# TensorE's order in a two-layer transformer kernel: products moved within both cross attentions, the second attention and the first experts

## The chip, the core and the metric

The kernel runs on one core of a Trainium2 chip. The core's engines are TensorE (PE; PEld is its weight load), VectorE (DVE), ScalarE (ACT), GpSimd (POOL) and SyncE (SP, which here only starts transfers). Each follows its own list of instructions and waits on semaphores for the others. The metric is the device time of one execution in microseconds; fewer is better.

## The reference

Eight sequences of 100 tokens with 256 channels pass through two layers. `ctx` has 361 rows per sequence; gates are tanh of one number each.

```python
# layer 0
x = x + tanh(g_xattn[0]) * cross_attention_0(layernorm(x), ctx)   # 16 heads of 64; query i sees the keys j with j % 100 == i
x = x + tanh(g_ffn[0]) * block_0(layernorm(x))                     # self attention, then experts, each with a residual
# layer 1
x = x + tanh(g_xattn[1]) * cross_attention_1(layernorm(x), ctx)   # 16 heads of 16, all keys
x = x + tanh(g_ffn[1]) * experts_1(layernorm(x))                   # 8 experts, best 2 of the distances to 8 centroids

def block_0(x):
    x = x + attention(rmsnorm(x))          # causal, 16 heads, latent keys of 32, rotated half
    p = softmax(rmsnorm(x) @ Wgate + bias) # 8 experts, best 2, weights normed
    return x + shared(rmsnorm(x)) + sum_e comb[:, e] * (silu(x@Wg[e]) * (x@Wu[e])) @ Wd[e]
```

Where accuracy asks for it, the kernel splits a float32 factor in a high part (rounded to fp32r) and the low rest, and adds three products: high by high, high by low, low by high.

## The kernel before

All is written out by hand, one function per engine; the order of an engine's instructions is the order of the Python loops. Tokens stand in columns, in two halves of 400 (four sequences each). PS is the PSUM, eight banks; `mm` (line 501) issues nearly every product of PE, so nearly all rows of PE name L501.

**First cross attention.** For each sequence b, `keys(b)` makes eight key tiles and `values(b - 1)` eight value tiles, six fp32r products each (`project_a`). DVE multiplies keys by queries (`products`, L1753), PE sums heads (`sim`), DVE and ACT make the softmax in six steps (`softmax_a`, L1761 to L1780, with `exps`, L1168, and `round_weights`, L1175, on ACT). Behind each value tile but ahead of the next, PE spreads the softmax weights over the tile's rows (SPREAD by SES); ACT copies the values (`vcopy`, L1185), DVE weighs them (`weigh`, L1792), POOL adds the keys' slots (L1529, L1532). The eight sums behind it are `project_out_a`, four groups of 24 products: one stands between `values(6)` and `values(7)`, three follow.

**Second attention.** 16 steps (8 sequences by 2 groups of heads): scores (`qk`), a softmax by DVE and ACT with POOL, transposes (`turn`, L672), the mixed values (`mix`) and ACT's copies of them (L1264). Then four groups of four float32 products, (half n, channels mo), project the output; each adds 1 to `b_output_summed`, and DVE adds it to Y (L1888). They read UT and WOA.

**First experts.** `norm(3)`, the router's scores (float32, 8 columns), then nine expert tiles by two halves, 18 steps: `up(i)` makes gate and up sides, six products each; ACT takes SiLU (L1292), DVE multiplies (`gate_up`, L1987) and weighs by the router's weight (L2006), ACT and DVE split the hidden part (HTH L1332, HTL L1963), `down(i)` makes six products. ACT rounds the weights of a tile (`split_hi0`, L1282), DVE takes the rest (`split_lo0`, L1952). The router's chain of some 20 short steps runs on DVE. Its result is transposed (L770) into WTS, spread over all rows by 16 products with UNIT, and copied out of four banks by ACT (even, L1321) and DVE (odd, L1994).

**Second cross attention.** The keys of a sequence are stored to HBM and come back head by head (KST). The queries are turned into that order by `stack_queries(n)` for half n, 16 products with PICK into three banks that ACT (`stack_even`, L1397) and DVE (`stack_odd`, L2071) empty. The loop over q from -2 to 32 has four steps of heads g per sequence b: scores (KST by QST), DVE's maxima (L2087), the transposed scores (QST by KST, 3 pieces), exps on ACT (L1369), `mix_v` (24 small products), and pieces of `project`, which makes later sequences' keys and values. In two places products on the weights alone stand ahead of `mix_v`: `fold_output` (eight float32 products with 8 columns or 1) at b = 4, g = 0, and `fold_centroids` (four such products, WO1T by the centred centroids, which DVE has made in the same step) at b = 5, g = 0; DVE reads both after the last step of that b.

**Second experts** follow with tokens sorted by expert; nothing in them is touched.

## Time and profile before

| what | value |
|---|---|
| three runs | 808.63, 802.99, 808.98 us (median 808.63) |
| profiled execution | 809.94 us, its span 808.1 us |
| mean granted clock of PE | 0.946 of full |
| PE busy | 724.1 us (90%) |
| DVE, ACT, POOL busy | 504.1, 380.6, 237.0 us |
| moved from and to HBM | 74.74 and 10.38 MB |

The span is the time from the first to the last instruction of the profiled execution, and the 1.8 us more lie around it. Busy times of engines overlap. The granted clock is the share of full speed that PE's clock had: 1.00 is 2.4 GHz, 0.50 is 1.2 GHz.

### The profile page before, as it was taken

The numbers are of one execution on the slowest core, as the hardware profiler recorded it, in microseconds if no ns is written. First come the engines' busy times: TensorE is split into PE (matmuls) and PEld (weight loads), VectorE is DVE, ScalarE is ACT, GpSimd is POOL, SyncE is SP. The second block draws the span as 40 slices with busy tenths as digits, with TensorE's granted clock in tenths as the row PEclk, the third lists the DMA queues.
The fourth block names the chain that finished last, engine by engine and source line by source line (L and its number), as shares of the span: only waits on it lengthen the run. The fifth ranks groups of instructions, "written<-read, shape, count | busy, mean of one in ns | idle before, by whom it ended". The sixth has DMA issues, their size and how long they took to land.

```text
span 808.1 us, 13459 instructions
## 1 busy us (share of the span) xinstructions
PE 724.1 (90%) x4735; PEld 603.7 (75%) x4735; DVE 504.1 (62%) x998; ACT 380.6 (47%) x828; POOL 237.0 (29%) x254
## 2 busy tenths in 40 slices
PE   6999999998989289989998899989994699999996
PEld 3578888888955178658996467667773699999995
DVE  3366666665339979537665666776786376665652
ACT  4513233322352169735434356665575256555561
POOL 0006655556205424600003402111200223243232
PEclk9999999999999789797999999998897599999999
DMA  6500000000060000000000776653233468999972
GB/s 236 212 2 20 18 20 20 18 2 0 15 270 1 0 1 2 2 1 0 1 10 1 170 150 167 144 134 95 84 141 125 135 217 307 306 328 295 327 219 58
DMA packets 30001, 85.97 MB, mean 106 GB/s; under 512 B 3913, under 2 KB 20425, under 8 KB 26609
## 3 DMA queue, kind: packets, MB, share of 16 engines
q1 hardware_dynamic: 26097, 79.88, 30.5%
q0 software_dynamic: 3840, 5.25, 3.1%
q8 instruction: 39, 0.64, 0.3%
q14 instruction: 25, 0.20, 0.1%
HBM read 74.74 MB, written 10.38 MB: 105 GB/s over the span
## 4 chain that ended last, share of the span: by engine, by line
PE 54%; DVE 12%; issue 4%; DMA 3%; ACT 2%; POOLq 0%; SPq 0%; DVEq 0%; ACTq 0%
PE PS L501 50%; DVE SM L2087 2%; PE PS L1073 2%; DVE WK L1849 1%; PE PS L672 1%; DVE WK L1846 1%; DMA XB<-token_rows,XROW 1%; DMA KST<-mask_rows 1%; DVE KTHL L2050 1%; PE PS L1043 1%; PE PS L889 1%; ACT RO L1246 0%; DMA out<-YO,TROW 0%; ACT SQ L1118 0%; DMA keys_by_head<-KTHL 0%
## 5 line engine op out<-in xcount | busy, mean ns | idle before, releaser
L501 PE MATMUL PS<-CTXH,WKV0H 128*128 128x362 f32 x256 | 87.1, 340 | 3.9 <-DVE PROD L1753 3.3
L2087 DVE TENSOR_REDUCE SM<-PS 100x1 f32<-100x362 f32 x128 | 64.5, 530 | 37.7 <-PE PS L501 36.9
L501 PE MATMUL PS<-CTXL,WKV0H 128*128 128x362 f32 x256 | 84.5, 330 | 0.0
L501 PE MATMUL PS<-CTXH,WKV0L 128*128 128x362 f32 x256 | 84.5, 330 | 0.0
L1369 ACT ACTIVATE WK<-PS 120x400 f32<-120x400 f32 (+1 forms) x96 | 48.3, 508 | 44.5 <-PE PS L501 43.6
L1792 DVE TENSOR_TENSOR RW<-PS,RW 128x400 f32<-128x400 f32 x64 | 36.8, 575 | 48.7 <-ACT RW L1185 32.9
L1185 ACT COPY RW<-PS 128x361 f32<-128x361 f32 x64 | 29.6, 463 | 66.8 <-PE PS L501 51.5
L1649 POOL DMA_INDIRECT out<-YO,TROW x20 | 31.7, 1583 | 100.0 <-DMA out<-YO,TROW 50.2
L501 PE MATMUL PS<-KST,QST 97*100 97x362 f32 x128 | 53.1, 425 | 7.9 <-DVE SM L2087 3.7
L501 PEld LDWEIGHTS PS<-CTXH,WKV0H 128*128 128x128 f32 x256 | 48.6, 190 | 12.9 <-DVE PROD L1753 6.6
L501 PE MATMUL PS<-RB,HTT 114*128 114x256 f32 (+1 forms) x240 | 55.2, 379 | 0.6 <-ACT HTT L1481 0.6
L1529 POOL TENSOR_TENSOR RW<-RW 128x200 f32<-128x200 f32 x64 | 39.4, 616 | 52.2 <-DVE RW L1792 49.8
L2150 DVE TENSOR_TENSOR GUL<-RB,GUH 128x1368 fp32r<-128x1368 f32 x28 | 44.2, 1578 | 14.3 <-ACT GUH L1407 14.3
L501 PE MATMUL PS<-GUH,XTH 128*128 128x342 f32 x160 | 51.7, 323 | 0.0
L501 PE MATMUL PS<-GUL,XTH 128*128 128x342 f32 x160 | 51.7, 323 | 0.0
L501 PE MATMUL PS<-GUH,XTL 128*128 128x342 f32 x160 | 51.6, 323 | 0.0
L1613 POOL TENSOR_TENSOR QST<-QALL,COLS 96x800 fp32r<-96x800 f32 x15 | 22.9, 1546 | 94.3 <-PE PS L501 84.8
L501 PEld LDWEIGHTS PS<-RB,HTT 114*128 114x128 f32 (+1 forms) x240 | 44.7, 189 | 6.2 <-ACT HTT L1481 0.9
L501 PEld LDWEIGHTS PS<-CTXL,WKV0H 128*128 128x128 f32 x256 | 49.1, 192 | 0.0
L501 PEld LDWEIGHTS PS<-CTXH,WKV0L 128*128 128x128 f32 x256 | 48.7, 190 | 0.0
L1753 DVE TENSOR_TENSOR PROD<-PS,RQ 128x400 f32<-128x400 f32 x64 | 36.4, 571 | 12.1 <-PE PS L501 11.2
L2310 DVE TENSOR_TENSOR STD<-PS,SIL 128x342 f32<-128x342 f32 x40 | 20.5, 511 | 32.2 <-PE PS L501 32.2
(328 smaller groups left out, 1863.0 us busy)
## 6 DMA issues: line engine op xcount, KB each, us to landing
RB<-W SPq DMA_DIRECT2D x14, 1368.0 KB, 5.9
RB<-W SPq DMA_DIRECT2D x20, 768.0 KB, 7.1
KST<-keys_by_head SPq DMA_DIRECT2D x24, 362.0 KB
RQ<-W SPq DMA_DIRECT2D x6, 1368.0 KB, 6.0
keys_by_head<-KTHL SPq DMA_DIRECT2D x8, 724.0 KB, 3.6
CTX<-ctxT SPq DMA_DIRECT2D x16, 361.0 KB, 6.5
RW<-WGU SPq DMA_DIRECT2D x1, 2304.0 KB, 8.5
RW<-WKV SPq DMA_DIRECT2D x1, 2048.0 KB, 9.9
```

The lines of the kernel that those rows point to most:

```text
L501: return pe.matmul(out, lhsT, rhs, start=start, stop=stop)
L1073: m = pe.transpose(PS[0:HT1, 5 + j, x * P:(x + 1) * P], H1T[:, j, x * HT1:(x + 1) * HT1], IDN[:, :])
L1185: act.copy(VSB[:, i % 3, 0:KV], PS[:, 4 + i % 2, 0:KV]).then_inc(sem["a_values_copied"], 1)
L1369: act.activation(PTC[0:CHT[c], q % 2, c, :], PS[0:CHT[c], 2 + c, 0:4 * S], ACT.Exp).then_inc(sem["c_exp_taken"], 1)
L1529: pool.tensor_tensor(pv[:, 0:2 * S], pv[:, 0:2 * S], pv[:, 2 * S:4 * S], ALU.add).then_inc(sem["a_halves_added"], 1)
L1613: pool.tensor_tensor(QST[b % 3][0:96, :, u, :], QALL[0:96, :, tok(b)].bitcast(F32), COLS[0:96, 21 + u:22 + u].unsqueeze(2).to_broadcast([9 ...
L1649: pool.indirect_dma_start(t["out"], bass.IndirectOffsetOnAxis(ap=TROW[:, k:k + 1], axis=0), YO[:, k % 2, :], None, compute_op=ALU.add).the ...
L1753: dve.tensor_tensor(out, k, q, ALU.mult).then_inc(sem["a_products_ready"], 1)
L1792: dve.tensor_tensor(PV[:, i % 3, :], PS[:, 6 + i % 2, 0:HALF], VSB[:, i % 3, :], ALU.mult).then_inc(sem["a_weighted"], 1)
L2087: dve.tensor_reduce(SM1[:, q % 2, j:j + 1], PS[0:S, i % 2, 0:KVE], AX_X, ALU.max, negate=True).then_inc(sem["c_maximum_found"], 1)
L2150: dve.tensor_tensor(GUL[k % 2][:, :, j, :], raw_gu(k, j), GUH[k % 2][:, :, j, :], ALU.subtract).then_inc(sem["expert_weights_low_ready"], 1)
L2310: dve.tensor_tensor(H1T[:, j, :], PS[:, 2 * j + 1, 0:HH], SIL1[:, j, :], ALU.mult).then_inc(sem["hidden_ready"], 1)
```

## The change

Six edits, none of which adds or removes a product. A product of the name `mm` in float32 stands as two records in the trace, one in fp32r as one.

1. *First cross attention*: the softmax steps of sequence 7 stand between DVE's weighings of sequence 6, from the third on, in place of behind all eight. ACT takes the exponential of sequence 7 after five of the eight copies of sequence 6.
2. *Second attention*: the two output groups of half 0 stand behind the transposes of the last two steps.
3. *First experts, ahead of the loop*: the weights of expert tile 0 are rounded before `norm(3)` on ACT, and their rest is taken between two of DVE's additions to Y; ACT rounds each half of XC when that half is there.
4. *First experts, spreading*: `up(2)` and `up(3)` are cut in their two sides, and a side of six products stands behind every fourth of the 16 spreading products.
5. *Second cross attention*: `stack_queries(1)` and the copies that go with it stand ahead of the loop's first scores.
6. *Second cross attention*: `fold_output` is cut in four pieces over the steps of b = 4, `fold_centroids` in two over the last two steps of b = 5.

```diff
+            def project_out_b(n, mo):
+                pe.wait_ge(sem["b_mixed_copied"], 2 * HB * (n + 1))
+                pe.wait_ge(sem["b_scores_shifted"], 2 * B - 1 + n)
+                pe.wait_ge(sem["b_exp_taken"], 2 * B - 1 + n)
+                for ti in range(4):
+                    m = mm(PS[:, 2 * n + mo, 0:HALF], WOA[:, ti, mo * P:(mo + 1) * P], UT[:, ti, half(n)],
+                           ti == 0, ti == 3)
+                m.then_inc(sem["b_output_summed"], 1)
+
             for i in range(2 * B + 4):
                 if i < 2 * B:
                     qk(i)
                 if 3 <= i < 2 * B + 3:
                     turn(i - 3)
+                if i in (2 * B + 1, 2 * B + 2):
+                    project_out_b(0, i - 2 * B - 1)
                 if i >= 4:
                     mix(i - 4)
-            pe.wait_ge(sem["b_mixed_copied"], 2 * B)
-            for n in range(2):
-                for mo in range(KD):
-                    for ti in range(4):
-                        m = mm(PS[:, 2 * n + mo, 0:HALF], WOA[:, ti, mo * P:(mo + 1) * P], UT[:, ti, half(n)],
-                               ti == 0, ti == 3)
-                    m.then_inc(sem["b_output_summed"], 1)
+            for mo in range(KD):
+                project_out_b(1, mo)
...
-                def up(i):
+                def up(i, sides=(0, 1)):
...
                     for c, name in enumerate(("gate_summed", "up_summed")):
+                        if c not in sides:
+                            continue
...
+                    if which == 0 and i % 4 == 3:
+                        up(2 + i // 8, (i // 4 % 2,))
                 for i in range(2, count + 2):
-                    if i < count:
+                    if (i > 3 or which) and i < count:
                         up(i)
...
                 project(1, part_)
+            stack_queries(1)
...
-                if (b, g) == (4, 0):
-                    fold_output()
-                if (b, g) == (5, 0):
-                    fold_centroids()
+                if b == 4:
+                    fold_output(g)
+                if b == 5 and g >= 2:
+                    fold_centroids(g - 2)
...
+            def fold_output(g):
+                if g == 0:
+                    pe.wait_ge(sem["c_aside_ready"], 2)
+                    pe.wait_ge(sem["c_operands_ready"], 3)
                 for k in range(KD):
...
+                    if g == 0:
+                        mm(PS[:, 6, 400:408], AVG[:, :], CENT2[:, k, :], k == 0, k == KD - 1)
+                    elif g < 3:
+                        mm(PS[:, 6, 407 + g:408 + g], WO1[:, k, 136 * g - 136:136 * g - 136 + P],
+                           COLS[:, 16 + k:17 + k], k == 0, k == KD - 1)
+                    else:
+                        mm(PS[0:S, 6, 416:424], ONES[:, 0:S], CENTSQ[:, k, :], k == 0, k == KD - 1)
+
+            def fold_centroids(c):
                 pe.wait_ge(sem["router_operand_ready"], 2)
                 pe.wait_ge(sem["moe1_small_loaded"], 32)
-                for c in range(2):
-                    for k in range(KD):
-                        mm(PS[:, 6, 400 + 8 * c:408 + 8 * c], WO1T[:, k, c * P:(c + 1) * P], CENTRED[k],
-                           k == 0, k == KD - 1)
+                for k in range(KD):
+                    mm(PS[:, 6, 400 + 8 * c:408 + 8 * c], WO1T[:, k, c * P:(c + 1) * P], CENTRED[k],
+                       k == 0, k == KD - 1)
...
                     project(2, 1)
-                    stack_queries(1)
                     project(0, 4)
                     project(0, 5)
...
-            def vcopy(b):
+            def vcopy(b, tis):
                 act.wait_ge(sem["zeros_set"], 1)
-                round_weights(b)
-                for ti in range(TI0):
+                for ti in tis:
...
-                vcopy(b)
+                round_weights(b)
+                vcopy(b, range(TI0 if b < B - 2 else 5))
+            exps(B - 1)
+            vcopy(B - 2, range(5, TI0))
+            round_weights(B - 1)
             outs_hi(B - 2)
-            exps(B - 1)
-            vcopy(B - 1)
+            vcopy(B - 1, range(TI0))
             outs_hi(B - 1)
             add_bias("a_output_summed", 0, 0, 0, "a_output_gated", [WK[:, i, :] for i in range(4)])
...
-            norm(3)
...
-                act.wait_ge(sem["b_output_summed"], 4)
+                if e:
+                    act.wait_ge(sem["b_output_summed"], 4)
                 for down in range(2):
                     act.copy(tile_of0("high", e, down),
                              tile_of0("raw", e, down)).then_inc(sem["expert_weights_high_ready"], 1)
+
+            act.wait_ge(sem["b_heads_mixed"], 2 * B)
+            split_hi0(0)
+            norm(3)
...
-                for n in range(2):
-                    act.wait_ge(sem["norm_done"], (6, 10)[which] + n + 1)
...
                 for n in range(2):
-
+                    if which == 0:
+                        act.wait_ge(sem["norm_done"], 6 + n + 1)
...
                 if which == 0:
-                    split_hi0(0)
                     split_hi0(1)
                 else:
...
+            stack_even(1)
             copies(2, 0)
-            stack_even(1)
...
-                if b:
-                    weigh(b - 1)
-            for step in range(6):
-                softmax_a(B - 1, step)
-            weigh(B - 1)
+                if 0 < b < B - 1:
+                    weigh(b - 1, range(TI0))
+            for ti in range(TI0):
+                weigh(B - 2, [ti])
+                if ti >= 2:
+                    softmax_a(B - 1, ti - 2)
+            weigh(B - 1, range(TI0))
...
+            def split_lo0(e):
...
             for i in range(4):
                 n, mo = divmod(i, 2)
+                if i == 2:
+                    split_lo0(0)
                 dve.wait_ge(sem["b_output_summed"], i + 1)
...
-                if which == 0:
-                    split_lo0(0)
-                else:
+                if which:
...
             keys_lo(1, 0)
             keys_lo(1, 1)
+            stack_odd(1)
...
             keys_lo(1, 0)
             keys_lo(1, 1)
+            stack_odd(1)
```

DVE at the end of the first cross attention, before: L1761 to L1780 are the six steps of the softmax (with SM and SES), L1792 the weighings of one sequence.

```order
L1761 TENSOR_REDUCE SM<-PS 128x100
L1766 TENSOR_TENSOR RW<-PS,SM 128x400
L1770 TENSOR_REDUCE SM<-RW 128x100
L1773 RECIPROCAL SM<-SM 128x100
L1776 TENSOR_TENSOR RW<-RW,SM 128x400
L1780 SCALAR_TENSOR_TENSOR SES<-SES,HS,RW 128x400
L1792 TENSOR_TENSOR RW<-PS,RW 128x400 x8
```

The same place now (L1776 to L1795 are the six steps, L1807 the weighings):

```order
L1776 TENSOR_REDUCE SM<-PS 128x100
L1807 TENSOR_TENSOR RW<-PS,RW 128x400
L1781 TENSOR_TENSOR RW<-PS,SM 128x400
L1807 TENSOR_TENSOR RW<-PS,RW 128x400
L1785 TENSOR_REDUCE SM<-RW 128x100
L1807 TENSOR_TENSOR RW<-PS,RW 128x400
L1788 RECIPROCAL SM<-SM 128x100
L1807 TENSOR_TENSOR RW<-PS,RW 128x400
L1791 TENSOR_TENSOR RW<-RW,SM 128x400
L1807 TENSOR_TENSOR RW<-PS,RW 128x400
L1795 SCALAR_TENSOR_TENSOR SES<-SES,HS,RW 128x400
L1807 TENSOR_TENSOR RW<-PS,RW 128x400 x8
```

The eight weighings in a row have become single ones, six of them with a softmax step behind.

PE behind the router in the first experts, before (WTS by UNIT spreads weights, XH and XL by WGU0 is `up`):

```order
L770 MATMUL PS<-IDN,RT 40x100 x8
L501 MATMUL PS<-WTS,UNIT 128x400 x16
L501 MATMUL PS<-XH,WGU0H 128x400
L501 MATMUL PS<-XL,WGU0H 128x400
L501 MATMUL PS<-XH,WGU0L 128x400
```

The same place now:

```order
L778 MATMUL PS<-IDN,RT 40x100 x8
L501 MATMUL PS<-WTS,UNIT 128x400 x4
L501 MATMUL PS<-XH,WGU0H 128x400
L501 MATMUL PS<-XL,WGU0H 128x400
L501 MATMUL PS<-XH,WGU0L 128x400
L501 MATMUL PS<-XH,WGU0H 128x400
L501 MATMUL PS<-XL,WGU0H 128x400
L501 MATMUL PS<-XH,WGU0L 128x400
L501 MATMUL PS<-WTS,UNIT 128x400 x4
```

The 16 spreading products stand in fours, with a side of `up(2)` or `up(3)` behind each four.

PE at the head of the loop in the second cross attention, as a difference (KST by QST are scores, CTX by RW is `project`'s keys, QCH and QCL by PICK is `stack_queries`):

```order
 L501 MATMUL PS<-QCL,PICK 96x400
 L501 MATMUL PS<-CTX,RW 128x361 x4
-L501 MATMUL PS<-KST_73,QST_76 100x362 x4
-L501 MATMUL PS<-CTX,RW 128x361 x2
 L501 MATMUL PS<-QCH,PICK 96x400
 L501 MATMUL PS<-QCL,PICK 96x400
...
 L501 MATMUL PS<-QCH,PICK 96x400
 L501 MATMUL PS<-QCL,PICK 96x400
+L501 MATMUL PS<-KST_73,QST_76 100x362 x4
+L501 MATMUL PS<-CTX,RW 128x361 x2
 L501 MATMUL PS<-RW,CTX 122x256 x4
```

The second stacking has moved ahead of the first four scores.

## Rows read from the trace of the kernel before

**Rows 1.** The page: PE clock granted, in tenths, in 40 slices of the span.

```profile
PEclk9999999999999789797999999998897599999999
```

**Rows 2.** Stretches at the low clock: length, busy (x instructions) by engine, clock, DMA.

```profile
198.60:202.00 3.40, 3.40 (x13) 3.40 (x12) 1.15 (x2) 0.93 (x2) 1.81 (x4) 0.50 0.00 0
...
335.10:345.40 10.30, 9.85 (x47) 5.22 (x46) 0.41 (x1) 3.14 (x8) 10.10 (x6) 0.50 0.00 1
...
372.70:379.50 6.80, 6.80 (x19) 5.73 (x19) 4.82 (x10) 3.35 (x8) 0.00 (x0) 0.50 0.00 0
```

**Rows 3.** Timeline, first cross attention: start, us, instruction [idle before <-releaser].

```profile
188.08 0.33 PE L501 MATMUL PS<-SES,SPREAD 128*128 128x362 f32 x1
...
189.26 0.33 PE L501 MATMUL PS<-SES,SPREAD 128*128 128x362 f32 x1
...
190.50 0.56 DVE L1761 TENSOR_REDUCE SM<-PS 128x100 f32<-128x400 f32 x1
...
197.25 0.44 PE L501 MATMUL PS<-SES,SPREAD 128*128 128x362 f32 x1 [2.28 <-DVE SES L1780]
...
207.08 0.33 PE L501 MATMUL PS<-SES,SPREAD 128*128 128x362 f32 x1
```

**Rows 4.** Timeline, end of the second attention, PE and DVE.

```profile
334.81 1.27 PE L672 MATMUL PS<-IDN,RO 100*100 100x100 f32 x8 [1.40 <-ACT RB L1258]
...
340.35 2.37 PE L501 MATMUL PS<-RO,RB 128*128 128x400 f32 x3 [0.45 <-ACT RO L1264]
...
345.81 0.57 DVE L1888 TENSOR_TENSOR Y<-PS,Y 128x400 f32<-128x400 f32 x1 [10.30 <-PE PS L501]
...
348.50 0.57 DVE L1888 TENSOR_TENSOR Y<-PS,Y 128x400 f32<-128x400 f32 x1 [2.11 <-PE PS L501]
```

**Rows 5.** Timeline, head of the first experts, PE and ACT.

```profile
359.50 1.62 ACT L1303 CAST XH<-XC 128x800 fp32r<-128x800 f32 x2 [1.29 <-DVE XC L1694]
...
362.94 0.70 PE L501 MATMUL PS<-XH,WGU0H 128*128 128x400 f32 x1 [1.89 <-DVE WGU0L L1952]
...
368.85 0.35 PE L770 MATMUL PS<-IDN,RT 100*40 100x100 f32 x2
```

**Rows 6.** Timeline, spreading and the first `down`, PE and DVE; last row: the chain.

```profile
370.04 5.43 PE L501 MATMUL PS<-WTS,UNIT 40*128 40x400 f32 x16 [0.32 <-ACT WTS L1318]
...
374.83 1.24 DVE L1994 COPY RQ<-PS 128x400 f32<-128x400 f32 x2 [0.19 <-PE PS L501]
...
380.04 0.42 PE L501 MATMUL PS<-HTH,WD0H 128*128 128x400 f32 x1 [0.34 <-DVE HTL L1963]
...
381.57 0.57 DVE L1963 TENSOR_TENSOR HTL<-WK,HTH 128x400 fp32r<-128x400 f32 x1
...
380.04 49.45 PE PS L501 x270
```

**Rows 7.** Timeline, head of the loop in the second cross attention, PE.

```profile
459.07 0.57 PE L501 MATMUL PS<-KST,QST 97*100 97x362 f32 x2 [3.06 <-DMA KST<-mask_rows]
...
462.06 1.07 PE L501 MATMUL PS<-QCH,PICK 128*96 128x400 f32 x1
...
466.77 1.89 PE L501 MATMUL PS<-RW,CTX 128*122 128x256 f32 x8
...
468.30 0.52 PE L501 MATMUL PS<-KST,QST 97*100 97x362 f32 x1
```

**Rows 8.** Windows between like steps (g = 3) of the loop, b = 3 to 7.

```profile
518.90:536.40 17.50, 15.69 (x166) 11.74 (x165) 12.82 (x35) 11.04 (x28) 3.00 (x2) 1.00 0.55 131
536.40:557.50 21.10, 20.04 (x181) 15.73 (x180) 12.81 (x35) 10.82 (x26) 3.00 (x2) 0.84 0.35 88
557.50:575.30 17.80, 16.75 (x166) 13.60 (x165) 12.58 (x37) 10.14 (x24) 8.03 (x6) 0.81 0.64 181
575.30:589.40 14.10, 12.63 (x157) 10.29 (x156) 11.62 (x34) 11.27 (x25) 0.00 (x0) 1.00 0.01 3
```

**Rows 9.** Timeline, `fold_centroids`, PE.

```profile
566.21 1.03 PE L501 MATMUL PS<-SQ 128*128 128x8 f32 x8 [0.73 <-DVE SQ L2130]
```

28 lines of the change are left out of this document (8 added, 20 removed).

## The prediction

> **What bounds the kernel now.** I read the clock row of the page first [rows 1]: PE is the engine that sets the time, and its clock is full nearly everywhere but in a few slices. The windows then show what these are: stretches of several us at 0.50, 1.2 GHz, in which PE is counted busy but does half the work [rows 2]. Then I read the timeline at each place that an edit touches, since what a change is worth is decided by the wait that ends last there.
>
> In the **first cross attention** PE stands for 2.28 us ahead of the first spreading product of sequence 7, whose weights DVE has only begun to make at 190.50 [rows 3]. A low stretch from 198.6 to 202.0 follows [rows 2].
>
> At the **end of the second attention** PE waits 1.40 us for the last transposes but one, and 0.45 us for the last copy of mixed values [rows 4]. From 335.1 to 345.4 its clock is low [rows 2], and the first output group, which starts at 340.35, is added by DVE only at 345.81, where the second follows after 2.69 us [rows 4].
>
> At the **head of the first experts** the first product waits 1.89 us for the weights' low rest, and the router's result is turned at 368.85 [rows 5]. Spreading takes 5.43 us, DVE's last copies from it run to 376.07, and the first `down` waits 0.34 us for HTL at 380.04; from there the chain is PE alone, 270 records in 49.45 us, 0.183 us each [rows 6].
>
> In the **second cross attention** PE stands 3.06 us until the keys are back from HBM, and the second stacking then takes it from 462.06 to 466.77 [rows 7]. In the loop, one sequence takes 17.5 us with key products for a later one at full clock and 14.1 us without; the two that hold the folds take 21.1 and 17.8 us at a mean clock of 0.84 and 0.81 [rows 8].
>
> **Part 1, first cross attention.** Without the wait the first spreading product could start 2.28 us ahead of 197.25, at 194.97. Eight tiles come 1.18 us apart at full clock (188.08 to 189.26), so the eighth would start 7 x 1.18 = 8.26 us later, at 203.2, where it now starts at 207.08 [rows 3]. That is 3.9 us, wait and low clock together. The cover: DVE's steps must end by 194.97. Before the change they take from 190.50 to 197.2, with ACT's two operations inside [rows 3]; started behind the third weighing (the eighth starts near 190.0, just ahead of 190.50; the third five tiles of 1.18 us before that, so it ends near 184.7), and with a weighing of some 0.6 us between each two, like the 0.56 us of a step on as many columns, they end by 184.7 + 6.7 + 5 x 0.6 = 194.4 at the worst, and less where they no longer wait for ACT's other work. Queued behind the waiting steps are DVE's weighings and behind ACT's exponential the last three copies of sequence 6; PE has two banks and waits for them only a tile later. If that cover fails, each late weighing costs PE up to 0.9 us, so I keep 3.0 to 3.9 and take 3.9. PE has no other wait up to the next norm that the shift would meet.
>
> **Part 2, second attention.** Two groups of 2.69 us stand earlier by two steps. They cannot fill the 1.40 us, since the transposes stand ahead of them; they fill the low-clock time behind. Before the change the dense work (four groups) starts at 340.35 and the clock is full from 345.4 [rows 2, 4], so 5.05 us of it run at half rate. If the same 5.05 us count from the end of the transposes, 336.08, the first group ends at 341.3, and what stands between now (4.3 us of transposes and mixing, 336.08 to 340.35, nearly all at half rate) needs about 2.2 us at full: 341.3 + 2.2 + 2.7 (second group) + 0.45 + 5.4 (half 1) = 352.0, against 345.7 + 3 x 2.69 = 353.8. If the low clock ends after 3.4 us, as in the first row of [rows 2], it is 2.6 us. I take 2.2, between 0 (the low clock goes on as long as now) and 3.0.
>
> **Part 3, weights of tile 0 and XH.** ACT stands 1.29 us ahead of XH for DVE's second half of XC [rows 5]. Before the change `up(0)` stands behind all of XH, weights of tile 0, XL and the weights' rest; with the weights done under the output groups (ACT is idle there, DVE waits 2.11 us between additions [rows 4] and the rest costs it about 1.1 us), it waits for the first half of XL alone. Next is then PE itself, whose router scores end at 362.94 - 1.89 = 361.05 [rows 5]: 1.9 us. DVE's router chain starts about 1.7 us earlier too, and PE's two `up` must be done: from 361.05, 24 products at 0.183 are 4.4 us, with a low-clock share up to 2.2 more, so the turning at 368.85 comes 1.3 to 1.9 us earlier. I take 1.6.
>
> **Part 4, spreading with products between.** This looks like the largest gain and I hold it for none. Before the change the path is: spreading from 370.04, last copy at 376.07, then 3.97 us of DVE and ACT (weigh, HTH, weights of tile 2, weigh, HTL) to `down(0)` at 380.04 [rows 6]. `up(2)` at half clock lies under that chain, free of cost. In the changed order the last four spreading products stand behind 18 products (3.3 us): 16 x 0.183 + 3.3 = 6.2 us, and their copies end 1.0 us later than now, at 7.1 from the start instead of 6.0. `down(0)` follows 3.97 behind, at 11.1 instead of 10.0. Behind it `down(1)` waits for HTL of step 1, which ends 2.1 us after `down(0)` starts (381.57 + 0.57 [rows 6]), and ends at 14.3. Before, `down(0)`, `up(3)`, `down(1)` are 24 records, 4.4 us, to 14.4. So moving 24 products out of the way is worth 0.1 us: what bound there was ACT's and DVE's chain. And PE now stands empty from 7.3 to 11.1, 3.8 us, more than the 2.28 us that preceded the low stretch of [rows 3]; a new low stretch as long as the shortest of [rows 2], 3.4 us, of which 2.1 us lie under the wait for HTL, costs 0.7 us, one of 6.8 us 2.4 us. I take -1.0, between -2.5 and +0.5.
>
> **Part 5, second stacking.** It leaves the loop's first step: 466.77 - 462.06 = 4.71 us. Its new place is the 3.06 us wait [rows 7], while ACT and DVE, which copy for it, are first busy with the last keys; by the 4.71 us (partly at half clock) it will overrun the keys' arrival by some 0.4 us. With the wait filled the clock should not drop. The keys come when they come: the transfer chain keeps its place relative to the norm. Next late in the first step is DVE's maxima. I take 4.2, between 2.5 and 4.7.
>
> **Part 6, folds in pieces.** The folds cost 21.1 - 17.5 = 3.6 and 17.8 - 14.1 = 3.7 us [rows 8], of which the second has 0.73 us of waiting for DVE's centroids and 1.03 us of its own [rows 9]; `fold_output` has twice as many products, so about 2 us. The remainder, about 1.6 and 2.0 us, is low clock. The wait goes, since the pieces stand two steps later. If the low stretches go too, and the pieces keep 1.6 (part of 2 fits in PE's 1.8 us of gaps, 17.50 less 15.69 [rows 8]) and 1.0 us, it is 3.6 - 1.6 + 3.7 - 1.0 = 4.7. Ends: 0.7 (only the wait) and 7.3 (all). A pointer for the middle: low stretches stand only where the folds do, and sequences with PE busy 12.63 of 14.10 us keep 1.00 [rows 8]. The Trainium skill, "TensorE: Matmul & The Clock Gate", section "A second HAM failure mode: psum-queue depth-cycling", speaks against it: small idle times between groups of matmuls in each iteration can be enough to make the clock swing between its levels, so pieces in six steps would be no better than one block in two. By that rule the part is worth 0.7, not 4.7. The rows of the unfolded sequences, with such gaps in each step and a clock of 1.00, don't bear it out so far.
>
> **Sum.** 3.9 + 2.2 + 1.6 - 1.0 + 4.2 + 4.7 = 15.6 us, on the profiled execution's 809.94 (span 808.1 and 1.8 around it): 794.3. That execution lies 1.3 us above the median 808.63 of the runs; on the median's level it is **793.0**. The runs differ by 6 us (802.99 to 808.98); a measurement of this kernel can tell about 1% from no change.
>
> **Rivals.** *The pieces keep the clock low.* Each piece adds time with hardly any columns to steps that have gaps already; low stretches come back in b = 4 and b = 5. Part 6 is then 0.7: 797.0. For it: both folds did it each time; against: the gaps alone don't.
>
> *The chains of DVE and ACT take what PE gives.* In the second attention the low clock lasts as long as now (part 2 is 0), and the hole behind spreading gives the long low stretch (part 4 is -2.5): 3.7 us less, 796.7. For it: part 4's chain is in the rows; against: only those two parts have it.
>
> *The pieces vanish in PE's gaps,* part 6 is 7.3: 790.4.
>
> *Slower: the first experts stay at half rate.* The 3.8 us hole lets the clock fall; a step of `down` and `up` is 18 records, 3.3 us at full clock and 6.6 at half. Each step at half costs 3.3 us, less what was waiting. From the fifth step on the 15.6 us are spent, with eight the time is 793.0 + 8 x 3.3 = 819.4, slower by over 1%; there are 14 steps. Against it: from 376 on the same dense products at half clock brought it back by 379.5 [rows 2, 6].
>
> **How the numbers follow.** Forecast 0.52; pieces keep the clock low 0.25; chains 0.13; pieces vanish 0.08; slower 0.02. All parts at their best give 3.9 + 3.0 + 1.9 + 0.5 + 4.7 + 7.3 = 21.3 us, 787.3 on the median's level; all at their worst but slower 3.0 + 0 + 1.3 - 2.5 + 2.5 + 0.7 = 5.0 us, 803.6, which needs all six at once. The range 787 to 801 holds the first four cases with the worst of two parts. Faster by over 1% is below 800.5: 0.89; within 1% 0.09; slower 0.02.
>
> **What would show it.** Right: no wait ahead of the first spreading product of sequence 7 and full clock behind it; the fourth addition to Y about 2 us nearer to the last scores; a hole of 3 to 4 us ahead of the first `down` with the clock low behind it; the loop's first step in about 4.7 us where it is 9.2; the windows of b = 4 and 5 near 19 and 15 us at 1.00. Wrong: a late weighing on DVE that makes PE wait in `values(6)`; scores of sequence 0 waiting for the stacking's copies; low clock in b = 4 or 5; a low stretch that has only moved elsewhere.

## The result, and the profile after

The changed kernel takes **795.25 us** (median of 6 runs, 794.09 to 796.55), the kernel before 808.81 in the same session (802.99 to 810.77): a ratio of 0.985, 95% interval [0.981, 0.989]. The profiled execution took 794.1 us (span 792.3). The two profiled executions lie 15.8 us apart, the medians 13.6.

The page of the changed kernel, PE's line and its clock [rows 1]:

```profile
PE 712.0 (90%) x4735; PEld 596.1 (75%) x4735; DVE 502.0 (63%) x998; ACT 379.9 (48%) x828; POOL 240.6 (30%) x254
...
PEclk9999999999999789998999999999996699999999
```

The windows of the changed kernel: first five stretches of low clock, then the two halves of the way from the first spreading product over the first `down` to the seventh `PS<-HTH,WD0H`, then the steps of the loop that answer to [rows 8]. Columns as in [rows 2]: length, busy (x instructions) of PE, PEld, DVE, ACT and POOL, then clock, DMA share, GB/s.

```profile
230.00:233.40 3.40, 3.40 (x6) 1.66 (x5) 0.00 (x0) 1.75 (x3) 0.00 (x0) 0.50 0.54 198
267.50:284.60 17.10, 5.88 (x32) 5.73 (x33) 12.34 (x25) 2.05 (x9) 3.52 (x3) 0.50 0.00 0
352.90:356.30 3.40, 3.40 (x12) 3.37 (x11) 2.70 (x13) 2.04 (x3) 0.00 (x0) 0.50 0.00 0
369.90:376.80 6.90, 4.84 (x14) 4.42 (x15) 5.63 (x12) 2.86 (x7) 0.00 (x0) 0.51 0.00 0
554.30:557.70 3.40, 3.40 (x32) 2.54 (x30) 2.25 (x7) 1.86 (x5) 1.40 (x2) 0.50 0.02 10
...
359.55:371.96 12.41, 9.02 (x41) 6.72 (x41) 7.46 (x15) 5.84 (x14) 0.00 (x0) 0.92 0.00 0
371.96:382.01 10.05, 10.05 (x42) 9.59 (x43) 6.63 (x13) 4.86 (x11) 0.00 (x0) 0.76 0.01 2
...
506.90:524.25 17.35, 15.71 (x167) 11.76 (x165) 12.73 (x35) 11.02 (x28) 3.00 (x2) 1.00 0.54 132
524.25:541.65 17.40, 16.28 (x175) 12.70 (x173) 12.82 (x35) 10.80 (x26) 3.00 (x2) 1.00 0.43 107
541.65:558.60 16.95, 15.02 (x166) 12.33 (x165) 13.00 (x37) 10.12 (x24) 7.99 (x6) 0.90 0.67 189
558.60:573.50 14.90, 13.38 (x166) 11.37 (x165) 11.67 (x34) 11.31 (x25) 0.00 (x0) 1.00 0.01 3
```

The timeline of the changed kernel at the places of [rows 3 to 7], and four rows of PE in the loop (COLS by RW are pieces of `fold_output`, SQ of `fold_centroids`):

```profile
188.52 0.33 PE L501 MATMUL PS<-SES,SPREAD 128*128 128x362 f32 x1
...
194.07 0.33 PE L501 MATMUL PS<-SES,SPREAD 128*128 128x362 f32 x1
...
202.28 0.33 PE L501 MATMUL PS<-SES,SPREAD 128*128 128x362 f32 x1
...
330.68 0.92 PE L672 MATMUL PS<-IDN,RO 100*100 100x100 f32 x8 [1.39 <-ACT RB L1270]
...
345.26 0.57 DVE L1913 TENSOR_TENSOR Y<-PS,Y 128x400 f32<-128x400 f32 x1 [2.11 <-PE PS L501]
...
358.36 0.86 PE L778 MATMUL PS<-IDN,RT 100*40 100x100 f32 x8
...
364.08 0.98 PE L501 MATMUL PS<-WTS,UNIT 40*128 40x400 f32 x4
364.99 0.45 PE L501 MATMUL PS<-XH,WGU0H 128*128 128x400 f32 x1
365.28 0.34 PE L501 MATMUL PS<-XL,WGU0H 128*128 128x400 f32 x1
365.46 0.35 PE L501 MATMUL PS<-XH,WGU0L 128*128 128x400 f32 x1
365.64 0.34 PE L501 MATMUL PS<-XH,WGU0H 128*128 128x400 f32 x1
...
366.28 0.99 PE L501 MATMUL PS<-WTS,UNIT 40*128 40x400 f32 x4
...
366.94 1.06 DVE L2011 COPY RQ<-PS 128x400 f32<-128x400 f32 x2 [1.14 <-PE PS L501]
...
368.73 0.53 ACT L1347 CAST HTH<-WK 128x400 fp32r<-128x400 f32 x1 [1.09 <-DVE WK L2023]
...
369.81 0.69 DVE L1905 TENSOR_TENSOR WGU0L<-RW,WGU0H 128x512 fp32r<-128x512 f32 x1 [1.11 <-ACT WGU0H L1293]
...
371.24 0.57 DVE L1982 TENSOR_TENSOR HTL<-WK,HTH 128x400 fp32r<-128x400 f32 x1
...
371.96 0.67 PE L501 MATMUL PS<-HTH,WD0H 128*128 128x400 f32 x1 [3.40 <-DVE HTL L1982]
...
451.57 0.49 PE L501 MATMUL PS<-KST,QST 97*100 97x362 f32 x2
...
454.75 1.89 PE L501 MATMUL PS<-RW,CTX 128*122 128x256 f32 x8
...
537.58 0.53 PE L501 MATMUL PS<-COLS,RW 128*128 128x1 f32 x4
...
542.96 0.53 PE L501 MATMUL PS<-COLS,RW 128*128 128x1 f32 x4
...
554.17 0.47 PE L900 MATMUL PS<-IDN,M 100*32 100x100 f32 x2 [0.92 <-DVE M L2115]
...
559.93 0.53 PE L501 MATMUL PS<-SQ 128*128 128x8 f32 x4
```

**How the traces are compared.** I took the start of one instruction on each side of every part, and held the length between them against the same length before. The signs are: the last spreading product of sequence 6 and of sequence 7; the last scores of the second attention (330.70 before, 326.57 after) and the fourth addition to Y; the router's turning; the first addition behind the experts (432.08 and 424.14); the first turning of maxima in the loop (468.82 and 456.80); the 57th and the 120th of DVE's 128 reductions of scores (523.78 to 592.95 and 511.77 to 577.02). That gives, in us:

```
                                   before   after    gain   predicted (ends)
1 spreading, seq 6 to seq 7         17.82   13.76    4.06    3.9 (3.0 to 3.9)
  up to the last scores            123.61  124.29   -0.68    -
2 last scores to 4th Y             23.17   18.69    4.48    2.2 (0 to 3.0)
3 4th Y to turning                  14.98   13.10    1.88    1.6 (1.3 to 1.9)
4 turning to 1st addition           63.23   65.78   -2.55   -1.0 (-2.5 to +0.5)
5 1st addition to maxima            36.74   32.67    4.07    4.2 (2.5 to 4.7)
6 57th to 120th reduction           69.17   65.25    3.92    4.7 (0.7 to 7.3)
```

With 0.74 us by which sequence 6 already ends sooner, where nothing was changed, and 0.08 lost in the lengths that the table leaves out, this is 15.8. The sum of 15.6 was met, but with two errors against each other, in parts 2 and 4. The -0.68 stands where nothing was changed either; the clock is low there for 20.5 us, 13.7 before: 3.4 us at 230.00, and 17.1 us from 267.5 on where it was 13.7. Which of the two costs it is not shown (with part 2 alone, in experiment 4, a stretch of 3.4 us from 235.5 on stands in the same length, and it takes 123.39). So before anything is explained, one must know how far such a length varies from one execution of the same code to the next. That, and part 4, are what the experiments are for.

### The profile page after: what moved, and what is told of

Same layout as the page of the kernel before. It is cut to its first block, busy times and chain, and to the rows that moved or that the text cites. A ratio compares the mean times of both kernels' runs of the same rounds, so it can differ in the third digit from the quotient of the medians.

```text
span 792.3 us, 13464 instructions
## 1 busy us (share of the span) xinstructions
PE 712.0 (90%) x4735; PEld 596.1 (75%) x4735; DVE 502.0 (63%) x998; ACT 379.9 (48%) x828; POOL 240.6 (30%) x254
## 4 chain that ended last, share of the span: by engine, by line
PE 73%; DVE 15%; issue 5%; ACT 3%; DMA 2%; SPq 1%; POOLq 0%; DVEq 0%; ACTq 0%
PE PS L501 69%; DVE SM L2105 2%; PE PS L1083 2%; DVE WK L1866 1%; DVE WK L1863 1%; PE PS L672 1%; SPq L363 1%; DMA XB<-token_rows,XROW 1%; DVE SM L1785 1%; DVE PROD L1768 1%; DMA RW<-WQ 1%; PE PS L1053 1%; DVE KTHL L2067 1%; PE PS L900 1%; DVE RW L1781 1%
## 5 line engine op out<-in xcount | busy, mean ns | idle before, releaser
L1807 DVE TENSOR_TENSOR RW<-PS,RW 128x400 f32<-128x400 f32 x64 | 36.8, 575 | 47.3 <-ACT RW L1194 33.7
L501 PE MATMUL PS<-KST,QST 97*100 97x362 f32 x128 | 51.5, 412 | 5.4 <-DVE SM L2105 4.2
L1768 DVE TENSOR_TENSOR PROD<-PS,RQ 128x400 f32<-128x400 f32 x64 | 36.4, 571 | 12.0 <-PE PS L501 11.1
L2326 DVE TENSOR_TENSOR STD<-PS,SIL 128x342 f32<-128x342 f32 x40 | 20.4, 511 | 32.2 <-PE PS L501 32.2
```

Source lines behind the costliest of these rows:

```text
L501: return pe.matmul(out, lhsT, rhs, start=start, stop=stop)
L1768: dve.tensor_tensor(out, k, q, ALU.mult).then_inc(sem["a_products_ready"], 1)
L1807: dve.tensor_tensor(PV[:, i % 3, :], PS[:, 6 + i % 2, 0:HALF], VSB[:, i % 3, :], ALU.mult).then_inc(sem["a_weighted"], 1)
L2326: dve.tensor_tensor(H1T[:, j, :], PS[:, 2 * j + 1, 0:HH], SIL1[:, j, :], ALU.mult).then_inc(sem["hidden_ready"], 1)
```

## Experiments

Each run lists the kernel before on the same chip beside it: 808.56 in the session of the first four, 809.83 in that of the next four, 810.00 in that of the last three. After all runs, the six lengths of every profile stand in one table at the end of this section.

**1. Part 4 undone.**

```
-                    if which == 0 and i % 4 == 3:
-                        up(2 + i // 8, (i // 4 % 2,))
-                    if (i > 3 or which) and i < count:
+                    if i < count:
```

> The changed kernel with part 4 undone: the sixteen spreading products stand in a row again, and up(2), up(3) stand behind them in the loop. In the changed kernel's trace the stretch from the turning to the first addition behind the experts takes 65.78 us where it took 63.23, so part 4 cost 2.55 us where I had -1.0. Theory: the cost is the hole of 3.40 us ahead of down(0) and the half clock behind it (369.9 to 376.8); without part 4 the first down comes about 10.0 us behind the first spreading product (12.41 with it), and the time is 795.25 - 2.5 = 792.7. Rival: the 2.5 us are chance of where the low clock falls, and the order is worth what I had reckoned: 794.2, with a first down 10.0 behind and low clock that costs as much as with part 4. A third: the half of the clock's drop that came in the old order too (372.7 to 379.5) shows again and lasts longer here, 795.5 or more.

Measured: 795.00 us (793.61 to 796.07), ratio 0.984 [0.980, 0.987]. The profile says that the old order is better: from the turning to the first addition 63.06 us, the first `down` 9.83 us behind the first spreading product. But the median is that of the changed kernel: of the 2.5 us that I had expected nothing shows in the times. The profile also shows where 1.65 us of it went: in the loop there is a low stretch at 485.50, in steps that hold no fold, with PE busy throughout.

```profile
485.50:489.00 3.50, 3.50 (x12) 2.77 (x11) 1.53 (x5) 0.00 (x0) 0.00 (x0) 0.51 0.54 214
```

**2. Part 4 kept, and the chain behind it started early.** DVE and ACT do the weighing, HTH and HTL of the first two steps and the split of tile 2 between the copies; their later loops leave out what is done by then (cut below).

```
 # DVE, in the loop over its copies
+                    if which == 0 and i in (1, 5):
+                        ...
+                        dve.tensor_tensor(HT[:, n, :], HT[:, n, :], weights_of(0, 0)[:, half(n)],
+                                          ALU.mult).then_inc(sem["hidden_weighed"], 1)
+                    if which == 0 and i in (3, 7):
+                        hidden_lo(i // 4)
+                    if which == 0 and i == 9:
+                        split_lo0(2)
 # ACT, in the loop over its copies
+                    if which == 0 and i in (2, 6):
+                        act.wait_ge(sem["hidden_weighed"], i // 4 + 1)
+                        act.copy(HTH[:, i // 4, :], HT[:, i // 4, :]).then_inc(sem["hidden_high_ready"], 1)
+                    if which == 0 and i == 6:
+                        split_hi0(2)
...
```

> The changed kernel, part 4 kept, but DVE and ACT do the first two steps' weighing, HTH and HTL and the split of tile 2 between the copies of the spreading, as soon as the first spreading weights are there, not behind all sixteen copies. If the hole ahead of down(0) is DVE's and ACT's chain that starts only behind the last copy, as the prediction says, then down(0) follows the last copies at about 8.4 us behind the first spreading product (12.41 in the changed kernel), 4.0 us sooner; the clock has no hole to fall in; at most 12.4 - 8.4 = 4.0 and another 1.5 for the low clock are gained: 795.25 - 4.0 = 791.3, with 789.7 at the best. Rival: DVE and ACT are full during the spreading (each has 8 copies of 0.5 to 0.57 us in 7.3), so the extra work delays the copies and with them PE's spreading by as much as is gained behind: the last spreading product starts 9 to 10 us behind the first (7.37 in the changed kernel) and the time stays at 795.3.

Measured: **791.89 us** (790.40 to 792.93), ratio 0.980 [0.976, 0.983]. In its timeline DVE weighs at 361.98, behind its first copy, and HTL is there at 363.71; the last group of spreading products starts 6.7 us behind the first, as in the changed kernel, and `down(0)` no longer waits:

```profile
361.98 0.57 DVE L2026 TENSOR_TENSOR WK<-WK,RQ 128x400 f32<-128x400 f32 x1
...
363.13 0.58 DVE L1989 TENSOR_TENSOR HTL<-WK,HTH 128x400 fp32r<-128x400 f32 x1
...
367.43 1.02 PE L501 MATMUL PS<-WTS,UNIT 40*128 40x400 f32 x4
...
369.58 0.34 PE L501 MATMUL PS<-HTH,WD0H 128*128 128x400 f32 x1
```

The first `down` stands 8.88 us behind the first spreading product instead of 12.41, no low clock lies there, and the length of part 4 is 60.32 us. The rival (the copies are delayed by as much) is out: both engines had the room. In the same session the order without part 4 took 795.00 us.

**3. Part 6 undone.** `fold_output` and `fold_centroids` in one block each, at (4, 0) and (5, 0), as before.

> The changed kernel with part 6 undone: fold_output in one block at (4, 0), fold_centroids at (5, 0). From like step to like step, b = 3 to 7 took 17.50, 21.10, 17.80, 14.10 us before (70.5) and 17.35, 17.40, 16.95, 14.90 in the changed kernel (66.6): part 6 gained 3.9 us. Theory (the blocks start the low clock, the pieces don't): windows near 21 and 18 us again with a mean clock near 0.8, 795.25 + 3.9 = 799.2. Rival (where the clock falls is chance, and the blocks themselves cost little): the windows of b = 4 and 5 come out near 18.5 and 16, at most 0.7 to 1.5 us slower, 796.0 to 796.8.

Measured: 797.27 us (795.58 to 799.81), ratio 0.986 [0.983, 0.990]; its profiled execution took 799.55. The windows of b = 4 and 5 in its profile, with two low stretches (536.6 to 540.0 and 557.1 to 563.9):

```profile
525.50:544.70 19.20, 17.72 (x178) 13.39 (x176) 12.28 (x33) 10.82 (x26) 3.00 (x2) 0.91 0.34 77
544.70:562.00 17.30, 15.93 (x167) 12.96 (x165) 12.23 (x36) 10.14 (x24) 8.01 (x6) 0.86 0.72 207
```

The length of part 6 is 68.57 us for 65.25: the blocks cost 3.3 in this pair, and 3.8 by the means of the table below (69.27 of four old lengths, 65.49 of nine new ones). The time lies between the theory's 799.2 and the rival's 796.0 to 796.8, and so do both windows, between 21 and 18.5 and between 18 and 16; so neither stands as I wrote it. What the profile does show is the low clock back where the blocks are.

**4. The kernel before with part 2 alone.** `project_out_b` as in the change, nothing else.

> The kernel before with part 2 alone: the two output groups of half 0 behind turns 17 and 18. In the changed kernel the last addition to Y came 4.48 us nearer to the last scores than before (18.69 us behind them where it was 23.17), where I had 2.2 with 3.0 as the best. Theory: the whole low stretch of 10.3 us at the end of the second attention goes when the groups stand there, so the part is worth 4.5 by itself: 808.8 - 4.5 = 804.3, and the last addition comes 18.7 us behind the last scores at full clock. Rival: my own reckoning, the low stretch stays and is only shorter, the excess in the changed kernel was where the clock happened to fall: 808.8 - 2.2 = 806.6, with a low stretch of 3.4 to 6.8 us between the last scores and the last addition.

Measured: 807.11 us (804.35 to 810.32), ratio 0.999 [0.996, 1.002]: alone it can't be told from no change by the time. The length is 20.32 us for 23.17 before, with one low stretch in it:

```profile
334.40:337.90 3.50, 3.50 (x12) 2.51 (x13) 0.57 (x1) 1.37 (x4) 3.35 (x2) 0.51 0.01 2
```

That is my own reckoning (2.2, here 2.85) and not the 4.48 of the first profile. Of the 2.85 us the next length gives 1.08 back (16.06 us for 14.98), with 6.8 us of low clock in it for 3.4.

**5. The changed kernel again.**

> The changed kernel itself once more, beside the others on one chip, as the measure of how far its clock varies from run to run. Theory: where the clock falls is partly chance. Then the ledger of this second profile agrees with the first to 0.1 us in the stretches without low clock, and differs by 1.5 to 2 us where a stretch of 3.4 us at half clock comes or doesn't: in the end of the second attention (part 2 gave 4.5 us in three profiles of this code and 2.8 in one), behind the spreading (part 4 cost 2.5 and 3.8), and in the loop. The median is 795.3 within 1 us. Rival: the stretches stand where they stood (230, 267 to 285, 353, 370 to 377, 554, 602 to 629), and the ledger is the same throughout within 0.3 us.

Measured: 796.94 us (794.53 to 802.68), ratio 0.986 [0.981, 0.991], 1.7 us above the first median and not within 1 us. The rival falls. The low stretch at 230 is not there, the one behind the spreading lies at 372.7 instead of 369.9, and the length of part 4 is 67.03 us for 65.78 by the same code.

**6. The early chain without the products between.** Experiments 1 and 2 together.

> The early weighing of the second experiment, but with the sixteen spreading products in a row and up(2), up(3) in the loop as in the kernel before. It tells what of the 3.4 us of the second experiment is the early chain alone. If the chain of DVE and ACT was all that mattered and the order of PE nothing, it runs as fast, 791.9. My theory: both are needed. In a row the spreading is held by the copies with the weighings among them (8 copies and 4 operations of 0.57 us on DVE, some 7 us), PE has nothing to do meanwhile, and 12 products (2.2 us) stand ahead of down(0) and 12 more ahead of down(1): the first down comes some 9.3 us behind the first spreading product (8.88 and 9.83 with the chain early and products between, and with neither), and down(6) 1.5 to 2.5 us later than there: 793.9. Rival: no better than with neither change, 795.0.

Measured: 797.24 us (796.02 to 798.38), ratio 0.986 [0.982, 0.990]. I had said 793.9: missed. The first `down` comes 11.65 us behind the first spreading product, later than in the old order (9.83), with the clock low for nearly all of it (362.1 to 372.4):

```profile
361.07:372.72 11.65, 11.00 (x29) 7.70 (x29) 7.76 (x16) 6.17 (x14) 0.00 (x0) 0.56 0.00 0
372.72:382.55 9.83, 9.83 (x55) 9.82 (x55) 6.17 (x12) 4.54 (x10) 0.00 (x0) 1.00 0.01 3
```

So neither half of experiment 2 is worth anything alone: products between without the early chain leave a hole, the early chain without them leaves PE with 16 thin products in the time of the copies.

**7. The kernel before with part 1 alone.**

> The kernel before with part 1 alone (softmax steps of sequence 7 between the weighings of sequence 6, ACT's exponential behind the fifth copy). Theory: the wait of 2.28 us and the low stretch of 3.4 us behind it both go by it, the eighth spreading product of sequence 7 stands 4.06 us nearer to that of sequence 6, as in the changed kernel (13.76 us for 17.82), and this is kept to the end: 808.6 - 4.1 = 804.5. Rival: the place is gained, but the low clock comes elsewhere (the norms and the head of the second attention took back 0.7 us of it in the changed kernel's trace) and only the wait is kept at the end: 808.6 - 2.3 = 806.3, or less.

Measured: 805.19 us (798.36 to 809.82), ratio 0.995 [0.992, 0.999]; the length is 13.76 us for 17.82, its profiled execution is 4.0 us shorter than the one before, and its median 4.6 us below the 809.83 of its session. The theory holds: the gain is kept, though later lengths also differ by up to 1.6 us either way. The end of the second attention is in the old order here and took 21.60 us, with this stretch in it, where it had 10.30 us of low clock [rows 2]:

```profile
331.80:338.60 6.80, 6.36 (x37) 3.35 (x30) 0.00 (x0) 2.26 (x6) 6.63 (x4) 0.50 0.00 1
```

**8. Part 5 undone.** `stack_queries(1)`, `stack_even(1)` and `stack_odd(1)` at their old places.

> The changed kernel with part 5 undone: stack_queries(1) in the loop's first step. From the first addition behind the experts to the maxima's first turning the changed kernel takes 32.66 us, the kernel before 36.74: 4.08 us. Theory: 795.3 + 4.1 = 799.4, the wait for the keys of 3.06 us is back with a low stretch of 3.4 us behind it. Rival: the stacking costs 3.1 us wherever it stands and the wait hides it either way only if the clock holds; without a low stretch the difference is 3.1 us, 798.4. If the whole is lost again later in the loop to low stretches that come anyway, 797 or less.

Measured: 801.04 us (800.10 to 807.51), ratio 0.990 [0.986, 0.994]; the length of part 5 is 37.97 us for 32.67, with a low stretch from 457.9 to 464.7. It is worth its 4.1 and more. The profiled execution was the slowest of its seven (807.51), and in part for another reason, in code that is the same as the changed kernel's:

```profile
362.30:382.80 20.50, 18.22 (x49) 14.41 (x49) 9.81 (x19) 7.40 (x16) 0.00 (x0) 0.50 0.00 1
```

This is the slower rival in small: the clock fell during the spreading, 14.1 us ahead of the hole (2.28 us here), stayed low over the hole and came back 4.1 us behind the start of the first `down`, at the end of the second, where the rival needed five steps of `down` and `up`. Part 4 took 70.47 us. That the hole kept the clock low is not shown.

**9. The hole filled.**

```
+                        if which == 0:
+                            for _ in range(18):
+                                mm(PS[:, 0, 0:HALF], XH[:, 0, 0:P], XH[:, 0, half(0)], True, True)
```

> The changed kernel with 18 products more on PE, XH by itself into a bank that down(0) overwrites, between the wait for the last spreading copies and down(0); nothing reads them. They stand in the hole of 3.40 us (18 x 0.183 = 3.3 us) and do no useful work. It parts the two costs of the hole: the time in which PE waits for DVE's chain, which stays, and the half clock behind it, which goes if it is PE's standing still that brings it. The stretch from the turning to the first addition behind the experts took 65.78, 67.03, 67.03 and 70.48 us in four profiles of this order and 62.8 to 63.2 in five of the old one. Theory: with the hole filled down(0) still follows 12.4 us behind the first spreading product, but at full clock down(6) follows it within 8.3 us (10.05 and 11.3), the stretch is 64.0, and the time is 796.1 (mean of the two medians of the changed kernel, 795.25 and 796.94) less 2 to 3: 793.6. Rival: the low clock comes from the thin spreading products ahead of the hole and not from the hole, the stretch stays near 67 and the time near 796.1. A second: the filling overruns the hole, each product costs 0.18 us, up to 1 us.

Measured: 794.60 us (792.57 to 795.23), ratio 0.982 [0.979, 0.985], with 3.3 us of work that nobody needs. The first `down` comes at the same 12.40 us, and what is behind it takes 8.90 us at full clock, for 10.05 and 11.33 in the changed kernel:

```profile
360.37:372.77 12.40, 12.26 (x59) 9.98 (x59) 7.45 (x15) 5.85 (x14) 0.00 (x0) 1.00 0.00 0
372.77:381.67 8.90, 7.98 (x42) 7.65 (x43) 6.54 (x13) 4.78 (x11) 0.00 (x0) 1.00 0.01 3
```

Part 4 is 64.61 us; I had said 64.0 and 793.6. With the hole filled no low clock stands there, in this one profile. Against it the low clock costs 1.2, 2.4 and 2.4 us in three profiles of the changed order, and 5.9 in experiment 8, where it had begun ahead of the hole. The later `down` itself costs 1.6 (64.61 less 63.04, the mean of the old order). By the medians the filling gains 1.5 us on 796.1, and the intervals overlap.

**10 and 11. Experiments 1 and 2 once more.**

> The first experiment once more (the changed kernel without part 4), since its profile and its times do not agree: by the stretch from the turning to the first addition (63.06 us for 65.78 to 70.48, mean 67.6) it should be 2.7 to 7.4 us faster than the changed kernel, by the medians it was 795.0 for 795.25. Theory: the profile is right and the order without part 4 is worth 4 us by itself; the other executions had one or two low stretches more in the loop (two of them cost 1.7 us each in unfolded steps of the loop, 485.5 to 489.0 in that profile), by chance: then this time the median is 792 to 793. Rival: without part 4 the low stretches behind it come in nearly every execution, so that the gain is given back in the loop: 795 again, and the loop shows a low stretch in a step without folds again.

> The second experiment once more (products between, weighing early), on the same chip as the two others of this call, to hold the fastest order against them. Expected: 791.9 within 1 us, the stretch from the turning to the first addition within 0.5 us of 60.31, and no low clock between 360 and 470. Rival: the 60.31 us were a lucky place of the low clock, as 65.78 was in the changed kernel against 70.48, and this profile shows 62 us or more and a median of 793.5.

Measured: 793.72 us (792.20 to 799.39), ratio 0.982 [0.978, 0.986], and **790.98 us** (788.74 to 792.91), ratio 0.978 [0.975, 0.981]. The plain order again has a low stretch of 3.4 us in steps of the loop without folds (521.1 to 524.5), so both theories of its expectation hold in part: the place is worth some 4.4 us in the profiles (63.22 for 67.58, the means of two and four), and some of it is lost again in the loop. In the same session the early chain is 2.7 us faster than the plain order (3.1 in that of the first four). It gave 60.33 us for part 4, to 0.01 us the same as at first.

The lengths in all profiles, in us, worked out as above from the starts in each timeline ("old" is a part that stands as in the kernel before; "PE old" has PE's old order in part 4, but the early chain):

```
                        1      2      3      4      5      6
before                17.82  23.17  14.98  63.23  36.74  69.17   all old
4 groups only         17.82  20.32  16.06  62.76  37.17  70.80   old: 1 3 4 5 6
7 first attention     13.76  21.60  15.95  62.78  38.06  68.55   old: 2 to 6
after                 13.76  18.69  13.10  65.78  32.67  65.25
5 again               13.76  18.70  13.11  67.03  32.67  65.92
3 folds in blocks     13.76  18.70  13.11  67.03  32.68  68.57   old: 6
8 stacking late       13.76  20.39  13.11  70.47  37.97  65.76   old: 5
9 hole filled         13.76  20.32  13.10  64.61  32.67  65.86
1 spreading plain     13.76  18.69  13.11  63.06  32.69  65.43   old: 4
10 the same           13.76  20.31  13.10  63.37  32.68  67.33   old: 4
2 weighing early      13.76  20.32  13.11  60.32  32.67  64.27
11 the same           13.76  20.32  13.10  60.33  32.67  64.27
6 early, plain        13.76  20.39  13.10  64.79  32.67  65.33   PE old: 4
```

## Why the prediction was right, and where its steps were not

The forecast case came about, 793.0 for 795.25 measured, within its range. That the sum of 15.6 met the 15.8 between the two profiles is luck in part: part 2 gave 2.3 us more there than its term and part 4 took 1.6 more, and the profiled execution of the changed kernel was its fastest (794.09 to 796.55), that of the kernel before 1.1 us above its median. Its terms, one by one:

**Part 1 was right** (3.9; 4.06 in eleven profiles without exception, 13.76 us for the 17.82 of both old ones). The cover held: the wait is gone (194.07 has none), and so is the stretch of low clock behind it.

**Part 2: the mechanism was right, and the size too, but the first profile alone would have told otherwise.** The term was 2.2, between 0 and 3.0, and that profile shows 4.48, beyond the end. The table shows why: the new order takes 18.7 us when no low clock lies in it (4 of 11 profiles) and 20.3 to 20.4 with one stretch of 3.4 us (7 of 11); the old order takes 21.6 with 6.8 us and 23.17 with 10.3. The first pair was the worst of the old and the best of the new. Means are 22.4 and 19.7: 2.6 us. My reckoning had counted the low time only as shifted; in fact there is less of it, by 3.4 us or more.

**Part 3 was right and a little short** (1.6; 1.9 by the first pair, 2.6 by the mean of the three old lengths, 15.66). Low clock costs nothing in the new length: 13.10 or 13.11 us in all ten profiles, eight with 3.4 us of it and two (experiments 6 and 8) with none. What binds is DVE's router chain: at full clock PE stands waiting for it, here in experiment 8.

```profile
360.08 0.87 PE L778 MATMUL PS<-IDN,RT 100*40 100x100 f32 x8 [1.45 <-DVE RT L1972]
```

**Part 4 failed, in two steps.** I had reckoned that the last spreading product starts 6.2 us behind the first ("16 x 0.183 + 3.3") and `down(0)` 11.1 behind it. The last one in fact starts 7.37 behind (its group at 6.73). Inside a group the spreading products on 40 rows soon follow as closely as the dense ones (the last three of the group at 364.08 start at 364.36, 364.55 and 364.72). What I had left out is the change between the two kinds: ten products, four thin and six dense, take 2.20 us (364.08 to 366.28), where 10 x 0.183 is 1.83, so each change costs about 0.19 us, and there are six up to the last group, 1.1 us.

The last copies end 8.45 us behind the first product (366.94 + 1.06 - 359.55), where I had 7.1. From there the chain takes 3.96 us, where I had 3.97, and the first `down` is at 12.41. The hole was to be 3.8 us and is 3.40. The second step is the clock behind it: I had 0.7 to 2.4 us for it and took about 1.1, and by experiment 9 it costs 1.2, 2.4 and 2.4 in three profiles (5.9 in experiment 8 holds more than the hole).

The old order has 3.4 to 6.8 us of low clock there in all of its five profiles too, but its lengths are 62.76 to 63.37: much of it lies under the chain of DVE and ACT. Together part 4 is -4.5 us by the means (67.58 for 63.04), and not -1.0; without experiment 8 it is -3.6. By medians it is less, 796.1 (mean of two) for 794.4: 1.7 us, with intervals that overlap, so that the times alone don't tell it from none. In the two profiles without part 4 one stretch of 3.4 us in the loop explains 1.65 us of the difference; whether it comes because of part 4's absence or by chance is open. That the order "looks like the largest gain and I hold it for none" was the right reading: the bound is the chain of DVE and ACT. What I didn't ask is whether the chain must begin so late and stand in that order. HTL needs only the weighed part and HTH, which ends at 369.26 (368.73 + 0.53); DVE starts HTL at 371.24, behind a wait of 1.11 us for the weights of tile 2, their rest and the second weighing. So 2.0 of the 3.40 us are DVE's own order; no run changes that alone. It needn't begin so late either, and started early the same interleaving turns from a loss of 4.5 us to a gain of 2.7 (60.32 for 63.04).

**Part 5 was right** (4.2; 4.1 to the first profile of before, 4.8 to the mean of the four old lengths, since the old place had low clock of 3.4 to 6.8 us each time). The copies overran the keys' arrival, as foreseen: the scores that waited 3.06 us for the keys [rows 7] follow the last stacking product at once, at 451.57, so the keys were there by then.

**Part 6: the mechanism was right in the main, the size 0.8 too large.** The window of 17.40 us holds the first two of `fold_output`'s four pieces (the second at 537.58) and is as long as the unfolded one (17.35), at 1.00: there they vanish. The next holds the other two and takes 16.95 with a low stretch at its end, and both pieces of the centroids (the first at 559.93) stand in the last, 14.90 for 14.10. 3.9 us in all. The rival *the pieces keep the clock low* is out at its price (0.7 for this part) and for b = 4: from the first piece on no profile with the pieces has low clock until the end of b = 5.

Half of its sign did come: a stretch of 3.4 us at the end of b = 5, behind the four pieces and ahead of the two, in seven of nine profiles (between 553.8 and 570.5). The two without it (weighing early) take 64.27 us there, the other seven 65.25 to 67.33. Whether the pieces bring it or the gaps of PE in these steps (0.92 us ahead of 554.17) is open. What I drew from the Trainium skill, "TensorE: Matmul & The Clock Gate", section "A second HAM failure mode: psum-queue depth-cycling", that small idle times between groups of matmuls can be enough to make the clock swing, does not show in the window of 17.40 us: PE is busy for 16.28 of it, and the clock is 1.00. For the end of b = 5 no run here decides it. And my own pointer was too good as well: "low stretches stand only where the folds do" was true of one profile. Steps without folds had one at 485.5, 488.4, 501.1 (twice) and 521.1 in others, and in the old order at 532.4 in experiment 4.

Last, the level. I set the sum of 15.6 against a profiled execution 1.3 us above the median. The medians moved by 13.6. The 795.25 is 2.3 us above the forecast, where the changed kernel's own two medians (795.25 and 796.94) lie 1.7 apart, so at most a part of it is the spread between sessions.

**The fastest version** is experiment 2: 790.98 and 791.89 us, where the changed kernel took 795.25 and 796.94 in other sessions, and its ratios to the kernel before ([0.976, 0.983] and [0.975, 0.981]) leave out 1 and meet the changed kernel's ([0.981, 0.989] and [0.981, 0.991]) at their ends alone. The two were not run in one session.

## What to carry to other kernels

When real products are put between thin ones, PE no longer waits for the copies, but what stands behind them is released by another engine's chain: move that chain forward in the same edit, or the gap and the half clock behind it cost more than the order gives. Count the changes between products of different rows too; here each cost about 0.19 us. Compare lengths between fixed instructions over several profiles before you explain one of them; a part of 4.5 us in one pair of profiles was 2.6 by the means of two old and eleven new, while the new lengths of the parts that remove a wait (1 and 5) came out the same to 0.02 us each time. Where PE can't be given real work in a hole, idle products can be cheaper than the hole: 3.3 us of them left the first `down` in its place, and the clock was full in the one profile taken.

## What was not expected of the hardware

The same instructions at the same place run at full clock in one execution and for 3.4 us at 0.50 in another: the end of the second attention took 18.7 us in four profiles and 20.3 to 20.4 in seven, with nothing between. Where PE sets the time, one stretch of 3.4 us costs 1.6 us: 20.32 less 18.69 there, and 56.60 less 54.95 from the first turning of maxima to the 57th reduction (four profiles with a stretch, nine without). At the end of b = 5 it costs 1.0 to 1.7 us in six profiles (65.25 to 65.92 less 64.27). Where DVE's chain binds it costs nothing: 13.10 us with and without in part 3. It also comes in steps in which PE is counted busy throughout (3.50 of 3.50 us from 485.50 on). The worst was 20.50 us at 0.50 around the spreading, in one of four profiles of that order. Products on 40 rows follow each other as closely as those on 128, 0.17 to 0.19 us apart, but a change from one kind to the other costs about 0.19 us; between products that all use 128 rows none is seen (the first `down` of experiment 2 starts 0.18 us behind the last product of `up`, at 369.58).
